# The second half of the expert token list, built inside the first expert's first chunk

## The reference: what is computed

```python
x = x + 0.5 * ffn(layernorm(x))        # mixture of experts
x = x + attention(layernorm(x))        # 16 heads, causal, an added tanh term in the scores
x = x + 0.5 * ffn(layernorm(x))        # the same mixture again

def ffn(x):                            # 8 experts, top 2, capacity 1280 slots per expert
    probs = softmax(x @ Wg)
    top_vals, top_idx = top_k(probs, 2)
    # each (choice, token) gets the next free slot of its expert; over 1280 it is dropped
    # gates = top_vals of the kept choices, normalised to sum 1
    hid = buf[e] @ W_in[e]             # 256 -> 1024, split in a and g
    out_e = (gelu(a) * g) @ W_out[e]   # 512 -> 256
    # each token sums its two experts' rows, weighted by the gates
```

## Time and profile before

| | |
|---|---|
| time of the profiled execution | 1552.77 us |
| its span in the profile | 1551.0 us |
| median of three runs | 1550.21 us |
| PE busy | 1437.4 us, 93% |
| DVE busy | 994.4 us, 64% |
| ACT busy | 719.2 us, 46% |
| POOL busy | 681.1 us, 44% |
| DMA | 206.48 MB, mean 133 GB/s |
| first mixture's first `up` matmul | 64.32 us |
| second mixture's first `up` matmul | 1189.67 us |

### The profile page before, as it was taken

The page is one execution under the profiler, slowest core; times in us unless marked ns, Lnnn a source line. Parts: engine busy times, 40 slices in busy tenths (PEclk is TensorE's granted clock), DMA queues, the critical chain, the costliest instruction groups (busy, mean ns, idle before and its releaser), DMA issues. The chain is left out here.

```text
span 1551.0 us, 25160 instructions
## 1 busy us (share of the span) xinstructions
PE 1437.4 (93%) x8872; PEld 1091.9 (70%) x8874; DVE 994.4 (64%) x2526; ACT 719.2 (46%) x1106; POOL 681.1 (44%) x654
## 2 busy tenths in 40 slices
PE   4699999999878899999999999999896999999998
PEld 3589889899866555555555555555565998898998
DVE  7756655555368576777777677886367566565554
ACT  5333333333263455555556565665473333333332
POOL 1365565664435442323333332225303655656644
PEclk9799999999989698989999999999987999999999
DMA  9454433442299866665656569562073444335432
GB/s 306 139 105 100 94 64 87 102 93 38 29 194 273 263 185 157 168 174 134 178 149 178 131 177 258 170 188 97 30 236 116 105 98 97 60 92 103 94 38 26
DMA packets 125509, 206.48 MB, mean 133 GB/s; under 512 B 24280, under 2 KB 86232, under 8 KB 122520
## 3 DMA queue, kind: packets, MB, share of 16 engines
q1 hardware_dynamic: 89032, 157.96, 36.3%
q0 software_dynamic: 30720, 38.46, 15.1%
q10 hardware_dynamic: 5648, 8.66, 1.9%
HBM read 123.22 MB, written 82.54 MB: 133 GB/s over the span
## 5 line engine op out<-in xcount | busy, mean ns | idle before, releaser
L2188 ACT ACTIVATE a_wts<-a_s_psum 128x1024 f32<-128x1024 f32 (+1 forms) x384 | 301.7, 810 | 218.3 <-PE a_s_psum L2323 216.3
L2060 DVE CUSTOM_DVE_ANT_0 a_m_psum<-a_m_psum,mask 128x256 f32<-128x256 f32 (+2 forms) x492 | 248.4, 519 | 140.7 <-PE a_m_psum L2289 130.4
L2289 PE MATMUL a_m_psum<-a_kp,a_qp 96*128 96x512 f32 (+1 forms) x735 | 275.9, 403 | 26.1 <-DVE a_parts L2060 17.4
L2289 PEld LDWEIGHTS a_m_psum<-a_kp,a_qp 96*128 96x128 f32 x735 | 142.4, 196 | 159.5 <-DVE a_parts L2060 81.0
L1997 POOL TENSOR_SCALAR_AFFINE_SELECT a_wts<-a_wts 128x512 f32<-128x512 f32 x128 | 78.2, 634 | 329.0 <-ACT a_wts L2188 328.8
L1032 ACT ACTIVATE e_act_a<-e_a_psum 128x512 f32<-128x512 f32 (+1 forms) x192 | 101.2, 527 | 259.4 <-PE e_a_psum L1111 259.4
L2323 PE MATMUL a_s_psum<-a_qp,a_kp 97*128 97x512 f32 (+2 forms) x768 | 213.8, 361 | 0.7 <-DMA a_qp<-stats 0.4
L949 DVE TENSOR_TENSOR e_hid<-e_act_a,e_g_psum 128x512 f32<-128x512 f32 (+1 forms) x192 | 114.7, 597 | 141.5 <-PE e_g_psum L1111 136.8
L243 POOL DMA_INDIRECT e_slots<-normalized,e_token x160 | 166.2, 1039 | 81.7 <-issue 47.5
L1130 PE MATMUL e_o_psum<-e_w_hi,e_h_hi 128*128 128x256 f32 x640 | 183.4, 287 | 0.0
L890 POOL DMA_INDIRECT out<-e_res,e_sum_row x80 | 126.5, 1582 | 126.5 <-ACT e_res L1044 113.1
(11 more groups left out here) (292 smaller groups left out, 2702.9 us busy)
## 6 DMA issues: line engine op xcount, KB each, us to landing
packs<-x_res SPq DMA_DIRECT2D x48, 512.0 KB, 5.9
e_w_raw<-in_W_in SPq DMA_DIRECT2D x16, 1024.0 KB, 6.6
a_qp<-packs SPq DMA_DIRECT2D x15, 1024.0 KB, 8.0
a_kp<-packs SPq DMA_DIRECT2D x15, 1024.0 KB, 14.0
e_w_raw<-in_W_out SPq DMA_DIRECT2D x16, 512.0 KB, 8.4
normalized<-r_xn SPq DMA_DIRECT2D x16, 512.0 KB, 4.4
attended<-a_o_sb ACTq DMA_DIRECT2D x32, 256.0 KB, 4.6
a_qp<-packs SPq DMA_DIRECT2D x15, 512.0 KB, 10.1
```

The costliest lines, as they stand in the source:

```text
L2060: nc.vector.tensor_tensor_reduce(products, products, c["mask"][:, QC - width:], 1.0, MASKED, ALU.add, ALU.max, top).then_inc(max_read, 1)
L2188: nc.scalar.activation(wts[(u * NS + s) % 2][:, j, 0:w], s_ps[q % 2][:, 0:w], ACT.Exp).then_inc(weighed, 1)
L2289: nc.tensor.matmul(m_ps[bank((n, h, z))][:, 0:stream], qp[n % NB][0:PACK, h, qt * P:(qt + 1) * P], kp[n % NB][0:PACK, h, first * P:first * ...
```

## The change

The late list's four pieces were made by all engines before the first expert was begun. Now:

- PE does pieces 0 and 1, then the turns of the first chunk, then piece 2, then `up(0)`; piece 3 stands inside `up(0)` behind the second quarter, ahead of the second chunk's turns.
- DVE makes the last columns (z = 3) behind `s_lo` of the first chunk instead of ahead of it. The 70 columns of tokens (`late_tokens`) come behind the first quarter of `hidden(0)`. `first_rest` moves from the head of `hidden(0)` to behind its third quarter, `rows_and_choices` to behind its fourth.
- ACT makes the last lanes behind `s_hi` of the first chunk.
- The late list's sums lie in another PSUM bank (`lg_ps[1]`), and `h_hi`, `h_lo` and `res` are allocated ahead of `s_hi` and `s_lo`, so that other buffers of `route` lie under those that are written first.

The counts of compute instructions stay as they were. The diff's core:

```diff
-        late_ps = lg_ps[0][:, 0:2 * LATE]
+        late_ps = lg_ps[1][:, 0:2 * LATE]
...
-            for z in range(1, PIECES):
+            for z in range(1, PIECES - 1):
                 late_columns(z)
-            dve.wait_ge(piece_read, 2 * PIECES)
-            tokens(slice(ST, SLOTS), late_ps[:, 0:LATE], late_ps[:, LATE:])
+
+            def rest():
+                late_columns(PIECES - 1)
+
+            def late_tokens():
+                dve.wait_ge(piece_read, 2 * PIECES)
+                tokens(slice(ST, SLOTS), late_ps[:, 0:LATE], late_ps[:, LATE:])
+
+            held["last_columns"], held["late_tokens"] = rest, late_tokens
...
+            for z in range(PIECES - 1):
+                late_lanes(z)
+            held["last_lanes"] = lambda: late_lanes(PIECES - 1)
...
+            for z in range(PIECES - 2):
+                late_piece(z)
+            held["last_pieces"] = [lambda z=z: late_piece(z) for z in range(PIECES - 2, PIECES)]
...
+        h_hi = [sb(f"h_hi{u}", [P, KF, 512], F32R) for u in range(2)]
+        h_lo = [sb(f"h_lo{u}", [P, KF, 512], F32R) for u in range(2)]
+        res = [sb(f"res{j}", [P, D]) for j in range(ST)]
         s_hi, s_lo = sb("s_hi", [P, KD, CAP], F32R), sb("s_lo", [P, KD, CAP], F32R)
...
-                    first_rest()
-                    rows_and_choices()
-                    hidden(0, {1: lambda: slots_lo(e, 1, chunks)})
+                    hidden(0, {0: held["late_tokens"], 1: lambda: slots_lo(e, 1, chunks), 2: first_rest, 3: rows_and_choices})
...
             slots_lo(0, 0, FIRST_CHUNKS)
+            held["last_columns"]()
             in_turn(nc.vector, body)
...
             slots_hi(0, 0, FIRST_CHUNKS)
+            held["last_lanes"]()
             in_turn(nc.scalar, body)
...
+                        if first and (ci, f) == (0, 1):
+                            held["last_pieces"][1]()
                         if f in between:
...
             transposes(0, 0, 0, 0, FIRST_CHUNKS, FIRST_SLOTS_IN)
+            held["last_pieces"][0]()
             in_turn(nc.tensor, body)
```

More of the change, by code:

```diff
@@ L702, in scalar, with late_lanes @@
             nc.scalar.activation(first_valued[:, :, 0:ST], is_first[:], ACT.Copy, scale=c["lane"][:, 0:1]).then_inc(lane_made, 1)
-            for z in range(PIECES):
+            def late_lanes(z):
                 act.wait_ge(is_made, z + 2)
@@ L814, in tensor, with late_piece @@
                     last.then_inc(piece_read, 1)
[L815 to L821, removed]
+            def late_piece(z):
+                pe.wait_ge(column_made, z + 2)
+                pe.wait_ge(lane_made, z + 2)
+                for kt in range(z * N, (z + 1) * N):
+                    last = nc.tensor.matmul(late_ps, is_within[z][:, kt % N, :], valued[z % 2][:, kt % N, :], start=(kt == 0), stop=(kt == NK - 1),
+                                            skip_group_check=True)
+                last.then_inc(piece_read, 1)
+            for z in range(PIECES - 2):
+                late_piece(z)
+            held["last_pieces"] = [lambda z=z: late_piece(z) for z in range(PIECES - 2, PIECES)]
         return {"sync": sync, "gpsimd": gpsimd, "vector": vector, "scalar": scalar, "tensor": tensor}
@@ L839, in experts @@
         hid = [sb(f"hid{u}", [P, 512]) for u in range(2)]
-        h_hi = [sb(f"h_hi{u}", [P, KF, 512], F32R) for u in range(2)]
-        h_lo = [sb(f"h_lo{u}", [P, KF, 512], F32R) for u in range(2)]
-        res = [sb(f"res{j}", [P, D]) for j in range(ST)]
         by_choice, both = [sb(f"by_choice{k}", [P, ST]) for k in range(TOPK)], sb("both", [P, ST])
```

## The result

| | before | after |
|---|---|---|
| median of 7 runs each | 1548.02 us (1541.91 to 1552.11) | 1561.13 us (1556.88 to 1567.26) |
| ratio after to before, 95% interval | | 1.0105 [1.0084, 1.0126] |
| profiled execution, its span | 1552.77, 1551.0 us | 1561.13, 1559.4 us |

The change makes the kernel 1.05% slower, 16 us with an interval of 13 to 20; forecast were 12.4 us. The ratio isn't the quotient of the two medians, which lie 13.1 us apart. The before was run again beside the after, so it has seven runs here and a median 2.2 us under that of the first three.

A forecast was written before the change was run, and what follows sets the result against it. PE, always busy from quarter 2 of the second chunk, was taken as the bound, carrying earlier delay through. Late load 4.3 plus clock 1.9 made 6.2 us per mixture, 12.4 for both: 1550.2 becomes 1562.6 us, range 1558.0 to 1568.5.

The forecast's parts named there:

- The start: Seam of list and experts: turns begin once the second gather lands, so the first `up` matmul comes 1.6 us earlier.
- Rival (c): Clock also low at the seam: half rate through turns, piece 2, `up(0)`, up to 1.9 us per mixture; 1565.5; chance 0.1.
- ACT's head: ACT's late lanes and table load delay the first gelu to about 3.55 us behind first `up`; that still fits.
- DVE's row: DVE's order in the first chunk: `first_rest` ends 10.1 us behind first `up`, before 1.08; the 1.6 us lead is spent.
- The load: Second expert's weights on SP: issued 7.4 us later, 6.3 us from issue to ACT, quarter 2 4.1 us late.
- (a): Rival: the load takes 7.5 and 8.3 us as in the rows, with the clock's fall; 1565.8; chance 0.15.
- (d): Rival: no pause ahead of quarter 2, which doesn't wait for the load; 1550, or 1547.0 if piece 3 is absorbed; chance 0.05.
- The clock: PE's 4.2 us pause ahead of quarter 2 drops the clock to half, costing 1.9 us per mixture.
- (b): Rival: the load is late but the clock doesn't fall; 8.6 us, 1558.8; chance 0.15.
- DVE's backlog: DVE's weights' subtraction (1.22 us) between two `hid`s in the second chunk costs quarter 3 another 0.2 us.
- free edits: The other PSUM bank and new order of buffers move addresses, not instructions; priced at zero.
- (e): Rival: tiles land only when the list is done, no gain at the seam, stall 5.9 us per mixture; 1565.8; chance 0.05.

The follow-up runs named there:

- e6: On top of e1, PE does late piece 2 ahead of the first chunk's turns instead of behind them; 1546.15 us, 1.0013 of the before.
- e4: The changed kernel with `first_rest` two quarters sooner, right behind the late tokens; 1548.84 us, 1.0046 of the before.
- e2: The kernel before with only `first_rest` moved, behind the third quarter of `hidden(0)`; 1563.21 us, 1.0111 of the before.
- e1: The changed kernel with only `first_rest` put back ahead of the first quarter of `hidden(0)`; 1550.8 us, 1.0029 of the before.
- e5: The changed kernel with 17 unused matmuls of 512 columns filling PE's pause ahead of quarter 2; 1562.26 us, 1.0107 of the before.
- e3: The kernel before with only the other PSUM bank and the new order of buffers; 1542.3 us, 0.9983 of the before.
- e7: The changed kernel with pieces 0 to 2 before the turns, piece 3 right behind; columns, lanes, `first_rest` as before, tokens behind it; 1552.31 us, 1.0051 of the before.
- e8: e7 with `first_rest` behind the tokens and `rows_and_choices`, so the second expert's load is issued later; 1545.16 us, 1.0008 of the before.

## Why the prediction was right, and where its terms were off

*What bounds the kernel*: right. M differs by up to 9 us between kernels, and what follows stays at 337.2 to 337.3 us.

*The start* is the step that failed. Forecast was U 1.6 us earlier, measured 0.46 and 0.81. The mistake was to give the turns 0.60 and piece 2 1.15 us, durations at full clock. In the after PE idles 2.07 / 1.72 us ahead of the turns, and does both at half: from the turns to `up` it takes 2.73 us in both mixtures, forecast 2.0. The rest is that the turns began later behind the list's start, 0.5 us in the first mixture, where the second gather was issued at 57.93 and the turns started 3.36 us behind it, and 0.1 in the second. e6, without that idle time, gets 1.6 and 1.2, and e4's first mixture, with it but with the clock up, 1.4. Rival (c) had described this and I gave it 0.1, on top of the forecast; it happened at the seam in both mixtures, and in the first it reached into `up(0)`.

*Piece 3, ACT's head, DVE's row*: L1019 ended and SP issued at U + 9.80 in the second mixture, forecast U + 10.15. In the first it was U + 11.03, since `up(0)` ran partly at half clock there. That the lead would be spent even with an early load holds too: e6's M is the before's within 0.2 us.

*The load*: 6.61 and 6.39 us from issue to ACT, forecast 6.3, and 6.33 / 6.61 in e2. Taking the gathers' share off the measured 7.47 gave the right time, and (a) is out; but e4's 9.10 and 6.73 say that a sum by bytes doesn't hold for every load. The pause was forecast at 4.2 us and is 4.21 / 4.00; e1 and e2 show its cause from both sides. (d) is out: the issue would have had to come by U + 6.05, and e4 at U + 6.4 to 6.7 pauses in one mixture and not in the other. The Trainium skill (DMA: Bandwidth & Descriptors, Anatomy of one DMA) has a fit for transfers from POOL, and by it an estimate is 5.6 us; this load from SP is 0.7 to 1.0 longer in four readings, and the measurement decides.

*The clock*: it fell in both mixtures, so (b) is out. Forecast 1.9 each; by e5 it is 1.3 and 2.5, 3.8 together. Not as I had it was the time of the fall: not after 1.4 us of idle but as the work came back in the first mixture and about 1 us before that in the second, and half rate then lasted for 3.4 and 5.7 us of work. The two pauses, alike in length, differ twofold in price, so the 1.9 forecast for each was right only as their mean, and that is luck: nothing in my rows told the two apart. The Trainium skill (TensorE: Matmul & The Clock Gate, Part 1: The HAM clock gate) says that the gate runs on a clock of its own; the two readings agree with that, but nothing here shows the gate's own timing.

*DVE's backlog* was 0.3 instead of 0.2, *free edits* zero (e3). (e) is out: U did come earlier.

**The sum.** Forecast 6.25 per mixture; measured 8.08 and 7.32. Of the 2.9 us missed in both together, 1.9 lie at the start, 0.8 between U and quarter 2 (+1.1 in the first, -0.3 in the second), 0.2 behind it. The forecast of 1562.6 stands nearer to the measured 1561.13 than the sum deserves, by luck, because the first three runs of the before lay 2.2 us above its median of seven.

## What to carry to other kernels

When an instruction that a load waits for moves down its engine's row, follow the load to its user: it may be late by the whole move less the slack, and the loads' own durations must be taken with the company they will have. Such a load has a window, closed on the early side by the small gathers that it would hold back (e7) and on the late side by its first user (e2). Work put under an idle stretch of PE must be priced at the clock that the idle time leaves, and a gain of a few microseconds is read from a local stretch between landmarks, not from the whole time, when the rest of the program varies by ten.

## What the runs showed of the hardware that was not expected

- A load of 1.57 MB issued 1.05 us behind a gather of 128 rows held its tile back until 6.5 us after issue; 2.7 and 2.0 us behind it (e8) it did no harm. An issued gather isn't safe from a later load. The trace of the kernel before had this already: its gather issued at 1189.68, the load 1.09 us behind it, landed 6.5 us after issue. It serves the third chunk, and nobody waited for it.
- The granted clock held at 1.00 and 0.87 through pauses of 4.21 and 4.00 us, and was at half for the work behind them. The cost, 1.3 and 2.5 us, doesn't follow the pause's length. e2's pauses of 3.91 and 4.20 us ended the same way (0.50 over 81.20 to 84.50 and over 1207.60 to 1214.30), while 2.17 us in e4 left the clock at 1.00.
- An idle 1.6 to 2.4 us ahead of the turns, while the clock is still at half, goes with a late rise. In the four kernels that have it (after, e1, e4, e5) the granted clock reached full 8.7 to 12.1 us behind the list's start in seven of eight mixtures, and 4.4 us behind it in one, e4's first. In the six that don't have it, it did so after 3.3 to 5.9 us.
- The attention takes 749.8 to 761.3 us in different executions with no instruction of it changed. In the two profiled here PE's busy time there is 691.80 and 684.49 us; the 7.3 between them are the whole difference, so it lies in the matmuls' durations and not in waits. Windows of before and of after, begun about 0.25 us ahead of the last `down` matmul:

```profile
419.90:1180.49 760.59, 691.80 (x4004) 0.93 0.64 173
```
```profile
428.20:1181.56 753.36, 684.49 (x4005) 0.94 0.64 174
```

The length goes with the granted clock of the stretch: 0.93 in the four executions of 758.7 to 761.3 us, 0.94 in the three of 752.7 to 757.2, 0.95 in the three of 749.8 to 752.5. What sets the clock there was not tried.
